# One 160-column product per token tile for the second norm's channels and the gate scores

## The reference, cut to what matters

```
x = x + conv_block(_ln_c(x))          # two convolutions of signs, batch norms, relu
t = _to_tokens(x)                     # 16*1024 tokens of 64 channels
n = _ln_t(t)                          # (t - mean) / sqrt(var + eps) over the channels
logits = n @ gate_w + gate_b          # 16 experts
top_probs, top_idx = top_k(softmax(logits), 2)          # made to sum to 1
t = t + sum over the two of weight * ((silu(n @ w1[e]) * (n @ w2[e])) @ w3[e])
x = _from_tokens(t, x)
```

## Time and profile before

| | |
|---|---|
| runs before, median (lowest to highest) | 498.39 us (496.86 to 498.42) |
| the profiled execution's own time | 498.73 us |
| its span | 496.8 us, 14231 instructions |
| PE busy | 450.0 us, 91% of the span |
| DVE busy | 439.4 us, 88% |
| ACT busy | 408.7 us, 82% |
| POOL busy | 295.5 us, 59% |
| chain that ended last, by engine | PE 51%, DVE 30%, ACT 8%, issue 5%, DMA 3% |

### The profile page before, as it was taken

The page is one execution under the profiler, slowest core; times in us unless marked ns, Lnnn a source line. Parts: engine busy times, 40 slices in busy tenths (PEclk is TensorE's granted clock), DMA queues, the critical chain, the costliest instruction groups (busy, mean ns, idle before and its releaser), DMA issues.

```text
span 496.8 us, 14231 instructions
## 1 busy us (share of the span) xinstructions
PE 450.0 (91%) x4186; PEld 384.2 (77%) x4186; DVE 439.4 (88%) x1248; ACT 408.7 (82%) x949; POOL 295.5 (59%) x380
## 2 busy tenths in 40 slices
PE   7998989999997627899999999999999999999972
PEld 6676767777774515798988988989899899998871
DVE  3776897997979998899998999999999999999973
ACT  5797878887885413899999999999999999999960
POOL 3200018777777777777777766666555555547571
PEclk9898979989987765999999999999999999999997
DMA  6993102022000024420223432224441525310054
GB/s 163 152 391 134 42 2 70 27 73 71 27 32 28 31 52 90 91 66 28 53 51 72 86 76 56 58 63 104 95 108 42 149 57 142 94 33 21 20 177 169
DMA packets 62664, 40.97 MB, mean 82 GB/s; under 512 B 50003, under 2 KB 54318, under 8 KB 62080
## 3 DMA queue, kind: packets, MB, share of 16 engines
q1 hardware_dynamic: 52784, 29.30, 23.8%
q0 software_dynamic: 8800, 8.94, 5.3%
q10 hardware_dynamic: 1008, 1.84, 1.0%
HBM read 21.46 MB, written 19.19 MB: 82 GB/s over the span
## 4 chain that ended last, share of the span: by engine, by line
PE 51%; DVE 30%; ACT 8%; issue 5%; DMA 3%; SPq 1%; POOL 1%; DVEq 0%; POOLq 0%; ACTq 0%
PE up L982 9%; PE up L984 8%; PE up L813 6%; PE turn L995 6%; DVE xs_lo L1530 4%; PE small L829 4%; ACT xc L713 4%; PE lines L1017 4%; DVE hidden L1604 3%; PE small L963 3%; DVE hidden L1609 2%; PE up L788 2%; DVE sq L1604 2%; PE up L799 2%; PE lines L1019 2%
## 5 line engine op out<-in xcount | busy, mean ns | idle before, releaser
L532 POOL DMA_INDIRECT results<-result,page_in x147 | 156.5, 1064 | 88.1 <-ACT xc L713 39.7
L515 POOL DMA_INDIRECT pages<-payload,slot_int x128 | 130.6, 1021 | 95.3 <-DVE slot_int L1431 57.5
L982 PE MATMUL up<-up_w,xs_hi 128*128 x588 | 139.0, 276 | 7.4 <-DVE xs_lo L1530 6.7
L984 PE MATMUL up<-up_w,xs_lo 128*128 x588 | 138.4, 275 | 0.0
L713 ACT ACTIVATE xc<-up,back_scales 128x512 f32<-128x512 f32 x147 | 107.8, 733 | 12.6 <-PE up L984 10.7
L982 PEld LDWEIGHTS up<-up_w,xs_hi 128*128 128x128 f16 x588 | 57.9, 98 | 19.0 <-issue 12.2
L1614 DVE TENSOR_TENSOR hidden_lo<-turn,hidden_hi 128x512 f16<-128x512 f32 x98 | 67.5, 688 | 1.6 <-ACT hidden_hi L726 0.6
L726 ACT ACTIVATE hidden_hi<-turn 128x512 f16<-128x512 f32 x98 | 65.1, 664 | 0.5 <-PE turn L995 0.5
L1604 DVE SCALAR_TENSOR_TENSOR hidden<-up,page_in,xc 128x128 f32<-128x128 f32 x196 | 59.4, 346 | 6.2 <-ACT xc L713 5.4
L984 PEld LDWEIGHTS up<-up_w,xs_lo 128*128 128x128 f16 x588 | 58.1, 99 | 5.4
L995 PE MATMUL turn<-ident,hidden 128*128 128x128 f32 x392 | 58.8, 273 | 0.0
(11 more groups left out here) (265 smaller groups left out, 978.4 us busy)
## 6 DMA issues: line engine op xcount, KB each, us to landing
pages<-x SPq DMA_DIRECT2D x4, 1332.0 KB, 11.1
page_in<-pages SPq DMA_DIRECT2D x147, 36.0 KB
page_in<-pages SPq DMA_DIRECT2D x147, 32.0 KB
x_in<-in_x SPq DMA_DIRECT2D x7, 512.0 KB, 4.4
out<-up_raw SPq DMA_DIRECT2D x5, 512.0 KB, 3.1
results<-result,page_in POOLq DMA_INDIRECT x147
up_raw<-in_L_ffn_w SPq DMA_DIRECT2D x4, 512.0 KB, 8.1
pages<-payload,slot_int POOLq DMA_INDIRECT x128, 2.2
```

The costliest lines, as they stand in the source:

```text
L515: pool.indirect_dma_start(out=pages, out_offset=bass.IndirectOffsetOnAxis(ap=slot_int[q % PAYLOADS][:, t:t + 1], axis=0), in_=payload[q % ...
L532: pool.indirect_dma_start(out=results, out_offset=bass.IndirectOffsetOnAxis(ap=page_in[g % LOADS][:, k, D + AT_TOKEN:D + AT_TOKEN + 1].bit ...
L982: pe.matmul(target, xs_hi[g % 2][:, k * P:(k + 1) * P], weights[:, bass.ds(e * 2, 2 * HID)], start=True, stop=False)
L984: last = pe.matmul(target, xs_lo[g % 2][:, k * P:(k + 1) * P], weights[:, bass.ds(e * 2, 2 * HID)], start=False, stop=True)
```

## The change

**One product in place of two.** `ident` and `gate_mat` become two parts of one tensor, `ident_gate`, 160 columns wide. For each of the eight blocks PE now makes one float32 product with the block as weights and `ident_gate` as the moving side (`turn_and_score`): 128 columns are the turned channels, 32 the gate's scores. The results lie in three banks (`seats`): blocks 0 to 2 in `turn[0]`, 3 to 5 in `turn[1]`, 6 and 7 in `small`. `turn_channels` makes the first six where the transposes stood, `last_channels` the last two where `gate` stood, still behind `var2_read`.

**Who scales what.** DVE scales the channels of blocks 0 to 2 (384 elements) and, behind `gate_ready`, those of blocks 6 and 7 (256). ACT scales those of blocks 3 to 5, six operations, and does so ahead of `copy(a)`. `score` scales three pieces (96, 64 and 96 elements), the last behind `channels_ready[1]`, ACT's signal that its six are done; `gate_read` comes with the last piece.

```
+        ident_gate = sb("ident_gate", [P, P + 2 * E], F32)
+        ident = ident_gate[:, 0:P]
+        gate_mat = ident_gate[:, P:P + 2 * E].rearrange("p (a e) -> p a e", a=2)
...
+        PITCH = P + 2 * E
+        seats = [turn[0][:, 0:3 * PITCH], turn[1][:, 0:3 * PITCH], small[:, 32:32 + 2 * PITCH]]
+        seats = [a.rearrange("p (j w) -> p j w", w=PITCH) for a in seats]
...
             # ACT, channels(q)
-                for j in range(TILES // 2):
-                    t = TILES // 2 + j
-                    last = act.activation(payload[q % PAYLOADS][:, t, 0:C], turn[1][:, j * C:(j + 1) * C], ACT.Copy,
-                                          scale=rstd[:, 1, t:t + 1])
+                for j in range(3):
+                    for half in range(2):
+                        t = 6 + 2 * j + half
+                        last = act.activation(payload[q % PAYLOADS][:, t, 0:C],
+                                              seats[1][:, j, half * C:(half + 1) * C], ACT.Copy,
+                                              scale=rstd[:, 1, t:t + 1])
                 last.then_inc(channels_ready[1], 1)
...
+                if 0 <= b < PAIRS:
+                    channels(b)
+                if a < PAIRS:
                     for c in range(CH):
                         copy(c, a)
-                if 0 <= b < PAIRS:
-                    channels(b)
...
             # PE, norm(c, q)
                 if q >= 2:
-                    pe.wait_ge(channels_ready[c], q - 1)
+                    pe.wait_ge(gate_read, q - 1)
...
+            def turn_and_score(j):
+                return pe.matmul(seats[j // 3][:, j % 3, :], xc2[:, j * P:(j + 1) * P], ident_gate[:, :],
+                                 start=True, stop=True)
+
             def turn_channels(c, q):
...
-                for t in range(TPC):
-                    j = c * TPC + t
-                    last = pe.transpose(turn[c][:, t * P:(t + 1) * P], xc2[:, j * P:(j + 1) * P], ident[:, :])
+                for j in range(3 * c, 3 * c + 3):
+                    last = turn_and_score(j)
                 last.then_inc(turned_ready, 1)
 
-            def gate(q):
+            def last_channels(q):
                 pe.wait_ge(var2_read, q + 1)
-                for j in range(TILES // 2):
-                    last = pe.matmul(gate_ps[:, j * 2 * E:(j + 1) * 2 * E], xc2[:, j * P:(j + 1) * P],
-                                     gate_mat[:, :, :].rearrange("p a e -> p (a e)"), start=True, stop=True)
+                for j in range(6, 8):
+                    last = turn_and_score(j)
                 last.then_inc(gate_ready, 1)
...
             # DVE, channels(q)
-                half = slice(0, TILES // 2)
-                dve.tensor_tensor(payload[q % PAYLOADS][:, half, 0:C],
-                                  turn[0][:, :].rearrange("p (t d) -> p t d", d=C),
-                                  rstd[:, 1, half].unsqueeze(2).to_broadcast([P, TILES // 2, C]), ALU.mult)\
-                    .then_inc(channels_ready[0], 1)
+                for i, n in ((0, 3), (2, 2)):
+                    if i:
+                        dve.wait_ge(gate_ready, q + 1)
+                    at = slice(6 * i, 6 * i + 2 * n)
+                    last = dve.tensor_tensor(
+                        payload[q % PAYLOADS][:, at, 0:C].rearrange("p (j a) d -> p j a d", a=2),
+                        seats[i][:, :, 0:P].rearrange("p j (a d) -> p j a d", a=2),
+                        rstd[:, 1, at].rearrange("p (j a) -> p j a", a=2).unsqueeze(3).to_broadcast([P, n, 2, C]),
+                        ALU.mult)
+                last.then_inc(channels_ready[0], 1)
...
             # DVE, score(q)
-                dve.tensor_tensor(logits[:, :, :], gate_ps.rearrange("p (t e) -> p t e", e=E),
-                                  spread(rstd[:, 1, :], E), ALU.mult).then_inc(gate_read, 1)
+                for i, n in ((0, 3), (2, 2), (1, 3)):
+                    if i == 1:
+                        dve.wait_ge(channels_ready[1], q + 1)
+                    at = slice(6 * i, 6 * i + 2 * n)
+                    last = dve.tensor_tensor(
+                        logits[:, at, :].rearrange("p (j a) e -> p j a e", a=2),
+                        seats[i][:, :, P:PITCH].rearrange("p j (a e) -> p j a e", a=2),
+                        rstd[:, 1, at].rearrange("p (j a) -> p j a", a=2).unsqueeze(3).to_broadcast([P, n, 2, E]),
+                        ALU.mult)
+                last.then_inc(gate_read, 1)
```

More of the change, by code:

```diff
@@ L96, in sem @@
             return ctx.enter_context(nc.semaphore(name))
-        ident = sb("ident", [P, P], F32)
+        ident_gate = sb("ident_gate", [P, P + 2 * E], F32)
+        ident = ident_gate[:, 0:P]
+        gate_mat = ident_gate[:, P:P + 2 * E].rearrange("p (a e) -> p a e", a=2)
         ident_b = sb("ident_b", [P, P], BF16)
@@ L114, in metaformer_kernel @@
         minus_half = sb("minus_half", [P, TILES], F32)
-        gate_mat = sb("gate_mat", [P, 2, E], F32)
         gate_bias = sb("gate_bias", [P, E], F32)
@@ L258, in metaformer_kernel @@
         var_ps = [small[:, n * TILES:(n + 1) * TILES] for n in range(2)]
-        gate_ps = small[:, 32:32 + TILES * E]
-        largest_ps = small[:, 32 + TILES * E:CW]
+        largest_ps = small[:, 32 + 2 * PITCH:CW]
         chosen_ps = lines[:, (TILES + 1) * LINES:(TILES + 1) * LINES + P].bitcast(BF16)
@@ L848, in turn_channels @@
                 if q == PAIRS - 1:
-                    pe.wait_ge(channels_ready[c], q)
-                for t in range(TPC):
-                    j = c * TPC + t
-                    last = pe.transpose(turn[c][:, t * P:(t + 1) * P], xc2[:, j * P:(j + 1) * P], ident[:, :])
+                    pe.wait_ge(gate_read, q)
+                for j in range(3 * c, 3 * c + 3):
+                    last = turn_and_score(j)
                 last.then_inc(turned_ready, 1)
-            def gate(q):
+            def last_channels(q):
                 pe.wait_ge(var2_read, q + 1)
-                for j in range(TILES // 2):
-                    last = pe.matmul(gate_ps[:, j * 2 * E:(j + 1) * 2 * E], xc2[:, j * P:(j + 1) * P],
-                                     gate_mat[:, :, :].rearrange("p a e -> p (a e)"), start=True, stop=True)
+                for j in range(6, 8):
+                    last = turn_and_score(j)
                 last.then_inc(gate_ready, 1)
@@ L902, in _ @@
                 if 0 <= b < PAIRS:
+                    if b == 0:
+                        pe.wait_ge(gate_in, 48)
                     for c in range(CH):
@@ L911, in _ @@
                 if 0 <= b < PAIRS:
-                    if b == 0:
-                        pe.wait_ge(gate_in, 48)
-                    gate(b)
+                    last_channels(b)
                 if 0 <= s < PAIRS:
```

## The result

The changed kernel took 509.22 us (median of four runs, 508.23 to 510.45) where the kernel before took 498.40: a ratio of 1.0225, interval 1.0194 to 1.0256, slower by about 11 us. The forecast was 503.0 with a range of 499.8 to 506.0: the sign was right, the size was less than half. In two later sets of runs the same kernel took 505.64 and 505.82 (ratios 1.0142 [1.0082, 1.0203] and 1.0106 [1.0052, 1.0160]), 6.0 and 6.2 us above the kernel before; one more execution of the last set, 510.75, fell into a slower state and is not counted. Some 6 us of the loss thus repeat.

What follows compares the result with a forecast made beforehand. The prediction took the first stage as bound by PE and DVE taking turns on the chain; 1.4 + 1.0 + 0.9 + 1.3 + 0 = 4.6 us on 498.73 gave 503.3, or 503.0 against the median, range 499.8 to 506.0.

Steps and rivals of the forecast that it cites:

- PE's clock falls once more: Rival: one more half-clock stretch like step 4's, at PE's place on the chain, costs 2.1 us: 505.1; chance 0.17.
- the wait of step 2: DVE's second channels operation waits for gate_ready with two searches queued behind it, delaying variance(0, 2) on PE: 1.4 us lost.
- last sign of being wrong: The forecast would be wrong if TensorE's half-clock stretches lay elsewhere by several us.
- Step 3: The score's last piece on DVE waits for ACT's six payload operations, late behind center(3): 1.0 us lost.
- Step 4: Same wait of the score's last piece for ACT's six, with PE at half clock: 0.9 us lost.
- Steps 5, 7, 8, 9: DVE reaches the score's last piece after ACT ends, so only DVE's added 0.33 us each counts: 1.3 us together.
- Step 6: ACT about one us late, covered by DVE's 1.83 us wait for PE; PE's 0.4 eaten by the late score: 0.
- The mechanism of the two DVE waits: DVE waits for PE's last blocks and ACT's six, plus 0.33 us a pair: 501 to 505, chance 0.52.
- PE's 0.42 us a pair: Sixteen 160-column passes with hidden loads take 2.16 us on PE instead of 2.58, saving 0.42 us a pair.
- The rival in which it counts in all steps: PE sets the pace in all eight steps and its saving wins 3.4 us: 495.0; chance 0.06.
- The claim that a microsecond of the first stage moves the end by one: The second stage begins when the last pair is routed, so a first-stage microsecond lost or won moves the end about one.

Runs made afterwards that it cites:

- the kernel before with the wait: Kernel before, with one added DVE wait for the gate's products before the two searches in step 2: 502.85 us, ratio 1.0073.
- PE kept busy: Changed kernel with eight idle-time products added on PE in step 2, between conv(1) and variance(0, 2): 500.04 us, ratio 1.0025.
- the kernel with the moved searches: Changed kernel with step 2's two searches moved between DVE's two channels operations: 502.35 us, ratio 1.0037.
- the kernel with both moves: Changed kernel with DVE's step 2 searches between its two channels operations and ACT's six payload operations ahead of the squares: 499.13 us, ratio 1.0004.
- the padded kernel before: Kernel before with six, nine and six idle-time PE products at the ends of steps 2, 3 and 4: 499.98 us, ratio 1.0033.

## Why the prediction was wrong

**The step that failed** is the rival "PE's clock falls once more". The forecast took the wait of step 2 as 1.4 us and gave the clock a chance of 0.17 and a price of 2.1 us. But this wait brought the fall with it, in all five profiled executions in which it was left open: PE idle for 1.74 us (1.28 in the kernel before with the wait) inside a step that runs through PE alone. The price was also too small, as it took two products of step 4, when the wait stands ahead of three long ones: variance, convolution and `center2` took 2.38 + 2.58 + 3.34 = 8.30 us on the chain where they had taken 1.68 + 1.34 + 1.73 = 4.75 (the middle one by the 1.34 of the earlier trace rows), and the fall went on into step 3. In the profiled execution the clock cost 3.3 us in step 2 (20.57 less the 17.25 with PE kept busy) and some 1.6 in step 3 (2.57 less the 0.93 by which the kernel with the moved searches, which has as much half clock as the kernel before, exceeds it): 5.0 us, against 2.1 at a chance of one in six. In the sum itself the clock stood at nothing. The prediction's last sign of being wrong, half-clock stretches that lie elsewhere by several us, is the one that came true.

**The terms of the sum**, one by one:

- Step 2's wait: 1.4 forecast, 1.57 measured with the clock held. The idle time (2.5 forecast, 2.53) and the order behind it were right.
- Step 3: 1.0 forecast, 0.93 measured with the searches moved. Step 4: 0.9 forecast, 0.91 measured.
- Steps 5, 7, 8, 9: 0.33 each forecast. Steps 8 and 9 came to 0.32 and 0.34 (by the starts of `sided`, with which `weights` closes on DVE). Step 5 came to 1.22: I had DVE at the last piece later than ACT there, and it waited 0.91 us. Step 7 came to -0.66; the kernel before itself differs by more there from one profile to the next (19.53 and 18.21), so this is chance.
- Step 6: 0 forecast, 0.16 measured, with ACT late by 1.06 us and covered, as forecast.

These make 1.57 + 0.93 + 0.91 + 1.22 + 0.16 - 0.66 + 0.86 = 5.0 us for 4.6. The mechanism of the two DVE waits was right, and so were their sizes but for step 5; that the total comes so near is partly luck, since step 5's 0.9 too much is nearly met by the chance of step 7. The 0.86 is all that came on behind step 7. With the clock's 5.0, the start's 1.7 of chance and the second stage's -0.7 the 11 us are there. In the later sets the loss was 6.0 and 6.2 us; from the median of 498.39 that would be 504.4 to 504.6, inside the range and above the forecast by a part of the clock's share.

**PE's 0.42 us a pair** was right (0.41 in step 2 of the kernel with both moves). The rival in which it counts in all steps is out: with both waits gone the kernel was even with the one before, at 499.13, not 495.

**The claim that a microsecond of the first stage moves the end by one** held for the loss of the first result (11.7 us at `turn_rows`, 11.0 at the end). For what is won it holds only up to POOL's start in step 4, by the scatters and the page at 260 us, as the padded kernel before shows. The prediction did not see that page: its 0.84 us of idle time stands in the trace of before.

A passage of the Trainium skill bears on this (TensorE: Matmul & The Clock Gate, section "A second HAM failure mode: psum-queue depth-cycling"): it tells of another kernel, in which frequent short idle times of PE between groups of products made the clock go back and forth between its levels. The trace agrees in part: here it was one wait of 1.74 us, and work at 1.2 GHz behind it. I had read that page for transposes alone.

Why the score's last piece must wait for ACT at all, when both only read: by the Trainium skill (PSUM — Partial Sum Buffer, section "PSUM bank collisions raise a hardware error") two engines must not touch the same partitions of one bank at once, reads against reads included. No run here shows it; a kernel without that wait was not tried.

## What to carry to other kernels

A wait that lands on PE is priced with what runs behind it: look at how long the products behind the wait take at half clock, and count the fall in the forecast itself, not as a rival. When work is merged on one engine, look at what its consumers now have queued behind the new, later signal, on every engine that reads a part of it: here two long searches and six copies stood in the wrong order, and moving them gave back all of the loss. Where PE must wait, a few useless products in the gap may win back more than the wait cost, but this has to be measured each time: of the four kernels with such products here, two became faster, one showed no difference clear of noise and one lost 2 us.

## What the runs showed of the hardware

- PE's idle time of 1.28 to 1.75 us in step 2 was followed by work at 1.2 GHz in all five profiled executions that have it (of three kernels), and the same place filled with products ran at 2.4 GHz in two of two.
- Idle time is not all that counts. The next wait, 1.27 us at the end of step 2, was soon followed by a fall in nine of the eleven executions that left it open, and in two of the three that filled it. In the filled changed kernel, which left it open, the full clock followed: 1.48 us for the convolution at 48.12 us. What else brings a fall is not shown.
- The same start of the program differs by up to 2.3 us from one execution to the next (`x_ln` of step 0 from 14.33 to 16.62 us), with PE's first center between 1.89 and 3.07 us while the granted clock reads 1.00. The clock behind it has a part: all five late starts (16.60 to 16.62 us, two in the kernel before and its padded version, three in changed ones) have 6.8 us at half clock between 10 and 18 us, the other nine 3.4 us or none.
- A float32 product of 160 columns takes 0.135 us a pass behind hidden loads, 1.63 us for 12; the 32 more columns cost what 32 columns cost, and no load of their own.
